# Patch tokens by row: the patch projection of an image and text transformer with the patches as the stationary operand

## The chip, the cores and the metric

One NeuronCore of a Trainium2 chip runs the whole kernel. The metric is the device time of one execution in microseconds. Of the kernel before, three executions are given; their median is 570.28 us. The profile of one further execution has a span (first to last instruction on the core) of 532.9 us.

## The reference

```python
h = tok_ref(x, W, b, cls_token, pos_enc)         # 64 images, 36 patches each of 3 x 16 x 16 = 768 values
#   proj = patches @ W.T + b; out = concat([cls, proj]) + pos_enc     -> (64, 37, 256)
h = concatenate([h, txt], axis=1)                # txt (64, 77, 256)   -> (64, 114, 256)
h = h + attn_ref(layernorm(h))                   # linear attention, 16 heads: Q, K = elu(.) + 1
h = h + ffn_ref(layernorm(h))                    # 8 experts, each token goes to its best one
```

All is float32. The patch projection is the part that is changed; what comes after it reads its result, a token in a row of 256 values, from the tile rows_all.

## The kernel before, in words

**Precision.** A float32 product is made of three matmuls: both operands are split into a high part (a cast, mostly on ScalarE) and a low part, the rest (a subtraction on VectorE, `low`, L778). `product` (L1078 to L1080) multiplies high by high, high by low and low by high.

**Patch stage.** The 64 images are worked on eight at a time (OCT), 288 patches, and each eight in two units, which hold three chunks of 128 of the 768 features each. There are 16 units. In a unit a 128 x 128 block of the weight is stationary and 288 patches move past it, so a token comes out as a column: features on the partitions. For a unit, SyncE loads `x_in` (a ring of four), ScalarE casts to `xp_hi` (L625, a ring of two), VectorE makes `xp_lo` (L778), TensorE makes 18 matmuls, and after each second unit VectorE adds position and bias out of PSUM into `tokT_all` (`patches_out`, L817), by columns. The two units of one eight share their PSUM banks.

**Into rows.** The attention needs tokens by rows, 114 of one image on 114 partitions: 36 patches, the class token at row 36, 77 texts. For each pair of images GpSimd copies the patch columns from `tokT_all` to `tokT` (L540), TensorE turns them in four transposes into the bank `b_tok` (L1237), and ScalarE copies these to `rows_all` (L722). The texts come by DMA straight into their rows (`load_text`, L409).

**Attention loop.** It goes over 32 pairs of images, in steps; a step i holds pieces of the pairs i + 3 (turning the patch tokens) to i - 4 (the scatter). On each engine the order within a step is written out by hand in its `step(i)`, the same code for the first steps, a hardware loop over steps 8 to 23 unrolled by four, and the last ones. In a step: statistics of the first layer norm (VectorE, L834 and L840), its reciprocal root on GpSimd (`rstd`, L495 to L500), the normalised xn on ScalarE (L696), its transposes (L1148), K and V (`kvp`), Q, `k_in` (VectorE, L961), `k_neg`, `k_relu`, `k_exp` (ScalarE, L684 to L687), `k_sb` (GpSimd, L550), `kvm` (L1135), `apply` (L1120), `attn` (VectorE, L896), its transposes (L1111), the output product `wo`, the residual (VectorE, L873), statistics of the second norm, `rstd` again on GpSimd, xn on ScalarE (L667), its transposes (L1211), a copy `xn2T` (ScalarE, L704), the gate product (L1248), the choice of the expert and the rank of each token (L1195 to L1198), and two indirect DMAs by GpSimd, which write each token's row to its expert's region in DRAM (`scatter`, L521). From step 24 on, the experts' weights are split in the same steps (GpSimd L562). GpSimd's order in a step is: `so_far`, the copy to `tokT`, `rstd` of the first norm, `k_sb`, `rstd` of the second norm, `scatter`. TensorE's is: `kvm`, xn transposes, attention transposes, K and V, `wo`, `apply`, ranks, xn2 transposes, Q, the four transposes of patch tokens, the gate product.

**Early steps.** Steps -3, -2 and -1 prepare the first pairs; they stand between units of the patch stage, at places written out in the `units` lists.

**Queues.** SyncE's program is one list of DMAs and waits, all in order: weights of the projection, units, small tensors, constants, other weights, texts of the first pairs; then the remaining units, each behind a wait for its ring slot; then texts, each behind a wait on the statistics of two pairs before. GpSimd splits the attention weights during the patch stage (L572 to L582).

**After the loop.** A table of tiles by expert is made, and 64 tiles of 128 tokens go through their expert and are written to the output by indirect DMA. The change does not touch this part.

## Time and profile before

| what | us |
|---|---|
| median of the three executions | 570.28 |
| lowest, highest | 568.74, 573.35 |
| span of the profiled execution | 532.9 |
| TensorE matmul busy | 478.5 (90%) |
| VectorE busy | 394.3 (74%) |
| GpSimd busy | 348.1 (65%) |
| ScalarE busy | 335.1 (63%) |

The device time of the profiled execution itself is not listed apart from its span; the median lies 37.4 us above the span. A matmul record covers the passage through the array, so that records of successive matmuls overlap: work is read from the distance of their starts. The patch stage takes the first 52 us, the attention loop lasts until about 400, and the expert tiles take the rest.

### The profile page before, as it was taken

The numbers are of one execution on the slowest core, as the hardware profiler recorded it, in microseconds if no ns is written. First come the engines' busy times: TensorE is split into PE (matmuls) and PEld (weight loads), VectorE is DVE, ScalarE is ACT, GpSimd is POOL, SyncE is SP. The second block draws the span as 40 slices with busy tenths as digits, with TensorE's granted clock in tenths as the row PEclk, the third lists the DMA queues.
The fourth block names the chain that finished last, engine by engine and source line by source line (L and its number), as shares of the span: only waits on it lengthen the run. The fifth ranks groups of instructions, "written<-read, shape, count | busy, mean of one in ns | idle before, by whom it ended". The sixth has DMA issues, their size and how long they took to land. (4 is left out here: it accounts for less than half of the span.)

```text
span 532.9 us, 13968 instructions
## 1 busy us (share of the span) xinstructions
PE 478.5 (90%) x3686; PEld 445.1 (84%) x3687; DVE 394.3 (74%) x1324; ACT 335.1 (63%) x805; POOL 348.1 (65%) x727
## 2 busy tenths in 40 slices
PE   4999899999999999999999999999954499999991
PEld 4988789999898999989999988888843498989990
DVE  4666478888887888788878877877854288888881
ACT  4334467667666757766676776766632488888870
POOL 0463234677777677777777778887776067877774
PEclk9999899999999999999999999999995599999996
DMA  8951000111121112711111211110013567852220
GB/s 298 281 168 34 14 23 14 39 35 33 34 56 33 30 37 81 238 30 51 39 30 36 55 31 31 42 35 22 18 38 99 155 196 220 241 160 82 78 79 31
DMA packets 31578, 43.24 MB, mean 81 GB/s; under 512 B 8541, under 2 KB 23840, under 8 KB 31539
## 3 DMA queue, kind: packets, MB, share of 16 engines
q1 hardware_dynamic: 21650, 27.12, 17.4%
q0 software_dynamic: 9216, 15.12, 8.9%
q10 hardware_dynamic: 672, 0.53, 0.3%
q8 instruction: 18, 0.29, 0.2%
q14 instruction: 22, 0.17, 0.1%
HBM read 26.45 MB, written 17.17 MB: 82 GB/s over the span
## 5 line engine op out<-in xcount | busy, mean ns | idle before, releaser
L521 POOL DMA_INDIRECT sorted_rows<-rows,place x64 | 75.1, 1174 | 39.7 <-POOL place L516 28.7
L608 POOL DMA_INDIRECT out<-result,result_id x64 | 62.6, 978 | 30.2 <-DVE result L1059 13.7
L684 ACT ACTIVATE k_neg<-k_in 114x512 f32<-114x512 f32 x32 | 20.3, 634 | 59.7 <-DVE k_in L961 59.7
L1078 PE MATMUL b_kvp<-wkv_hi,xnT_hi 128*114 128x512 f32 x128 | 52.9, 413 | 0.0
L696 ACT ACTIVATE xn<-rows_all,shift,rstd 114x256 f32<-114x256 f32 (+1 forms) x64 | 34.9, 593 | 27.6 <-issue 24.2
L498 POOL TENSOR_TENSOR rstd<-ve,half_neg 114x2 f32<-114x2 f32 x64 | 47.0, 734 | 5.3
L1079 PE MATMUL b_kvp<-wkv_lo,xnT_hi 128*114 128x512 f32 x128 | 50.4, 394 | 0.0
L1080 PE MATMUL b_kvp<-wkv_hi,xnT_lo 128*114 128x512 f32 x128 | 50.2, 392 | 0.0
L495 POOL TENSOR_SCALAR ve<-mv 114x2 f32<-114x2 f32 x64 | 15.3, 239 | 53.2 <-DVE mv L840 29.3
L550 POOL TENSOR_TENSOR k_sb<-k_exp,k_relu 114x512 f32<-114x512 f32 x32 | 41.2, 1287 | 5.8 <-issue 4.4
L1078 PE MATMUL b_kvp<-wgu_hi,xsT_hi 128*128 x128 | 37.7, 294 | 6.3 <-DVE xsT_lo L778 6.3
L766 ACT ACTIVATE xs<-rows_all,affine 128x256 f32 (+1 forms) x64 | 39.1, 611 | 6.5 <-DVE affine L1066 6.5
L1135 PE MATMUL b_att<-v_sb,k_sb 114*128 114x136 f32 x256 | 38.5, 294 | 3.1 <-POOL k_sb L550 3.1
L1078 PE MATMUL b_qo<-wo_hi,attnT_hi 128*114 128x256 f32 x128 | 41.0, 320 | 0.0
L1078 PE MATMUL b_qo<-xnT_hi,wq_hi 128*128 128x256 f32 x128 | 38.7, 303 | 0.0
L667 ACT ACTIVATE xn<-rows,shift,rstd 114x256 f32<-114x256 f32 x64 | 35.1, 602 | 4.5 <-POOL shift L500 4.5
L1248 PEld LDWEIGHTS b_gate<-gate_s,xn2T 128*114 128x114 f32 x256 | 29.6, 187 | 9.7 <-ACT xn2T L704 9.1
L1080 PE MATMUL b_kvp<-wgu_hi,xsT_lo 128*128 x128 | 36.4, 284 | 0.0
L1079 PE MATMUL b_kvp<-wgu_lo,xsT_hi 128*128 x128 | 36.4, 284 | 0.0
L1248 PE MATMUL b_gate<-gate_s,xn2T 128*114 128x8 f32 x256 | 31.1, 248 | 5.7 <-ACT xn2T L704 5.7
L1080 PE MATMUL b_qo<-xnT_hi,wq_lo 128*128 128x256 f32 x128 | 36.0, 281 | 0.0
L1079 PE MATMUL b_qo<-xnT_lo,wq_hi 128*128 128x256 f32 x128 | 35.9, 281 | 0.0
(174 smaller groups left out, 1771.3 us busy)
## 6 DMA issues: line engine op xcount, KB each, us to landing
rows_all<-sorted_rows SPq DMA_DIRECT2D x64, 130.0 KB
rows_all<-in_x SPq DMA_DIRECT2D x16, 432.0 KB, 4.8
rows_all<-in_txt SPq DMA_DIRECT2D x32, 154.0 KB
rows_all<-in_wgu SPq DMA_DIRECT2D x8, 256.0 KB, 4.5
sorted_rows<-rows,place POOLq DMA_INDIRECT x64, 3.7
rows_all<-in_wdown SPq DMA_DIRECT2D x8, 128.0 KB, 4.7
out<-result,result_id POOLq DMA_INDIRECT x64
rows_all<-in_w_tok SPq DMA_DIRECT2D x2, 384.0 KB, 4.1
```

What stands on the lines that cost most here:

```text
L498: G.tensor_tensor(to[:, k, :], ve[:, 0, :], half_neg[0:TOK, :], ALU.pow).then_inc(chain, 1)
L521: G.indirect_dma_start(out=scratch[0:EXPERTS * REGION, :], out_offset=bass.IndirectOffsetOnAxis(ap=place[:, k, b:b + 1], axis=0), in_=rows ...
L550: G.tensor_tensor(k_sb[:], k_exp[:], k_relu[:], ALU.add).then_inc(k_ready, 1)
L608: G.indirect_dma_start(out=out, out_offset=bass.IndirectOffsetOnAxis(ap=result_id[:, k:k + 1], axis=0), in_=result[:, k, :], in_offset=Non ...
L667: last = S.activation(xn2[:, b, :], rows[:, k, b, 0:D], ACT.Identity, bias=shift2[:, k, b:b + 1], scale=rstd2[:, k, b:b + 1])
L696: last = S.activation(xn[:, b, :], rows_all[0:TOK, bass.ds(2 * p.n + b, 1), 0:D], ACT.Identity, bias=shift1[:, p.slot(2), b:b + 1], scale= ...
L766: S.activation(xs[:, t.slot(4)], rows_all[:, bass.ds(t.n, 1), 0:D], ACT.Identity, bias=affine[:, t.slot(4), 0:1], scale=affine[:, t.slot(4 ...
L1078: T.matmul(to, left_hi, right_hi, start=start, stop=False)
L1079: T.matmul(to, left_hi, right_lo, start=False, stop=False)
L1080: return T.matmul(to, left_lo, right_hi, start=False, stop=stop)
L1135: last = T.matmul(b_att[:, b, c * KVW:(c + 1) * KVW], k_sb[:, b, c * P:(c + 1) * P], v_sb[:, b, c, :], start=True, stop=True)
L1248: last = T.matmul(b_gate[0:TOK, b * EXPERTS:(b + 1) * EXPERTS], xn2T[:, k, b * TOK:(b + 1) * TOK], gate_s[:, k, :], start=(k == 0), stop=( ...
```

## The change

The operands of the patch projection change places. 128 patches (of three and a half images) are stationary and the 256 output features move, so a token comes out as a row. There are 18 units of 128 patches and all 768 features. VectorE adds position and bias out of PSUM into `patch_out`, a ring of four; the sum of position and bias by patch, in nine tiles that repeat, is made by GpSimd from a larger input `pos`. A tile of 128 patches isn't aligned with images, so each is stored to a table in DRAM, `patch_rows`, and read back by pairs of images to its rows in `rows_all`, beside the texts (`load_pair`). The class token's row is added once and written to all images by two DMAs (`cls_rows`). The copy to `tokT`, the transposes and the copy out of `b_tok` are gone, with `tokT_all`, `tokT` and their semaphores. In the early steps, -3 is gone. The host's layout of `x`, `pos`, `tok_b` and `cls` changes accordingly.

```diff
@@ -220,7 +220,7 @@
 
 
         staging = rows_all[:, TILES // 2:, :].rearrange("p t w -> p (t w)")
-        X_UNIT = (FC // 2) * OCT * PATCHES
...
@@ -347,9 +349,9 @@
         id_copied = sem("id_copied")
         stored = [sem(f"stored{k}") for k in range(4)]
 
-        SMALL_DMAS, WEIGHT_DMAS = 5, 5
+        SMALL_DMAS, WEIGHT_DMAS = 4, 5
         CONST_DMAS = 2
...
@@ -390,6 +392,11 @@
                 else:
                     what()
 
+        def patch_bank(t):
+
+            bank = (b_kvp, b_att)[(t.c // 2) % 2]
+            return bank[:, t.c % 2, 0:D]
+
...
@@ -402,44 +409,84 @@
                     sp.wait_ge(x_lo_ready, u.upto(4))
                 sp.dma_start(x_in[:, k * X_UNIT:(k + 1) * X_UNIT], x[bass.ds(u.n, 1)]).then_inc(x_loaded[k], 16)
 
-            def load_text(p):
+            def load_pair(p):
 
                 if p.had(2):
                     sp.wait_ge(mv1_ready, p.upto(2))
                 sp.dma_start(rows_all[CLS_AT + 1:TOK, bass.ds(2 * p.n, 2), 0:D],
                              txt[:, bass.ds(2 * p.n, 2)]).then_inc(s_in[p.slot(2)], 16)
-
+                sp.dma_start(rows_all[0:PATCHES, bass.ds(2 * p.n, 2), 0:D],
+                             patch_images[:, bass.ds(2 * p.n, 2)]).then_inc(s_in[p.slot(2)], 16)
+
+            def store_patches(t):
+
+                k = t.slot(4)
+                sp.wait_ge(patches_ready, t.upto())
+                sp.dma_start(patch_rows[bass.ds(t.n * P, P), :], patch_out[:, k]).then_inc(patches_stored[k], 16)
+
+            def stored_patches(t):
+
+                sp.wait_ge(patches_stored[t.slot(4)], 16 * t.rounds(4))
+
+            def cls_rows(n):
+
+                half = slice(n * IMAGES // 2, (n + 1) * IMAGES // 2)
+                sp.dma_start(rows_all[CLS_AT:CLS_AT + 1, half, 0:D],
+                             cls_row[:].rearrange("p (a d) -> p a d", a=1).to_broadcast([1, IMAGES // 2, D])
+                             ).then_inc(s_cls_rows, 16)
+
+            patch_images = patch_rows.rearrange("(i n) d -> n i d", n=PATCHES)
             W_HALF = FC // 2 * D
             sp.dma_start(w_tok_raw[:, 0:W_HALF], w_tok[:, 0:W_HALF]).then_inc(s_tokw, 16)
             load_unit(Turn(0, 0))
             sp.dma_start(w_tok_raw[:, W_HALF:], w_tok[:, W_HALF:]).then_inc(s_tokw2, 16)
             load_unit(Turn(0, 1))
-            for to, what in ((pos_s, pos), (tokb_s, tok_b), (cls_s, cls), (bq_s, bq), (gate_s, gate)):
+            sp.dma_start(tokb_s[:], tok_b.to_broadcast([P, D])).then_inc(s_pos, 16)
+            for n in range(POS_PARTS):
+                at = slice(n * POS_TILES // POS_PARTS, (n + 1) * POS_TILES // POS_PARTS)
+                sp.dma_start(posb[:, at], pos[:, at]).then_inc(s_pos, 16)
+                if n < 2:
+                    load_unit(Turn(0, 2 + n))
+            for to, what in ((cls_s, cls), (cls_pos_s, cls_pos), (bq_s, bq), (gate_s, gate)):
                 sp.dma_start(to[:], what).then_inc(s_small, 16)
-            for n in (2, 3):
-                load_unit(Turn(0, n))
+            load_unit(Turn(0, 4))
             sp.dma_start(con_s[:], consts).then_inc(s_const, 16)
             sp.dma_start(ids_s[:], ids).then_inc(s_const, 16)
-            load_unit(Turn(0, 4))
+            load_unit(Turn(0, 5))
+            store_patches(Turn(0, 0))
+            sp.wait_ge(s_cls, 1)
+            cls_rows(0)
             sp.dma_start(wkv_raw, wkv).then_inc(s_weights, 16)
-            load_unit(Turn(0, 5))
+            load_unit(Turn(0, 6))
+            store_patches(Turn(0, 1))
+            stored_patches(Turn(0, 0))
+            load_pair(Turn(0, 0))
+            load_unit(Turn(0, 7))
+            store_patches(Turn(0, 2))
+            stored_patches(Turn(0, 1))
+            load_pair(Turn(0, 1))
             sp.dma_start(wq_raw, wq).then_inc(s_weights, 16)
             sp.dma_start(wo_raw, wo).then_inc(s_weights, 16)
             sp.dma_start(bkv_s[:], bkv.to_broadcast([TOK, 2 * D])).then_inc(s_weights, 16)
             sp.dma_start(bias_row[:], bo).then_inc(s_weights, 16)
-            load_unit(Turn(0, 6))
-            for n in (0, 1):
-                load_text(Turn(0, n))
-            load_unit(Turn(0, 7))
-            with sp.Fori(2, UNITS // 4) as m:
-                for c in range(4):
-                    load_unit(Turn(m, c))
+            for n in range(8, PT):
+                load_unit(Turn(0, n))
+                store_patches(Turn(0, n - 5))
+            for n in range(PT - 5, PT):
+                store_patches(Turn(0, n))
+            sp.wait_ge(w_lo, 2)
+            sp.wait_ge(x_lo_ready, PT)
+            sp.wait_ge(weight_step, 6)
+            cls_rows(1)
+            for n in range(PT - 4, PT):
+                stored_patches(Turn(0, n))
+            sp.wait_ge(s_cls_rows, 32)
             for n in (2, 3):
-                load_text(Turn(0, n))
+                load_pair(Turn(0, n))
             BEFORE_EXPERTS = GU_STEP // 4 - 1
             with sp.Fori(1, BEFORE_EXPERTS) as m:
                 for c in range(4):
-                    load_text(Turn(m, c))
+                    load_pair(Turn(m, c))
             sp.wait_ge(h2_ready, RAW_PAIRS)
             for e in range(EXPERTS):
                 at = e * (GU + DOWN)
...
@@ -531,13 +578,6 @@
                         pool.wait_ge(rank_done, p.upto(1))
                     G.tensor_tensor(so_far[0:TOK, (p + 1).slot(2)], so_far[0:TOK, p.slot(2)], chosen[:, p.slot(2)],
                                     ALU.add).then_inc(so_far_ready, 1)
-                if (i + 3).within(PAIRS):
-                    p = i + 3
-                    until = ahead(pool, p.upto(1))
-                    pool.wait_ge(s_prep, 1)
-                    if p.had(1):
-                        pool.wait_ge(back_done, until)
-                    G.tensor_copy(tokT[:, :, :, 0:PATCHES], tokT_all[:, :, bass.ds(2 * p.n, 2), :]).then_inc(tokT_ready, 1)
...
@@ -562,9 +602,12 @@
                     G.tensor_tensor(wgu_lo[:, e].rearrange("p k d -> p (k d)"), expert_raw[:, at:at + GU],
                                     wgu_hi[:, e].rearrange("p k d -> p (k d)").bitcast(F32), ALU.subtract).then_inc(gu_lo_ready, 1)
 
-            pool.wait_ge(s_prep, 1)
-            pool.wait_ge(patches_ready, 1)
-            step(Turn(0, -3))
+            pool.wait_ge(s_pos, 16 * (POS_PARTS + 1))
+            for n in range(POS_PARTS):
+                at = slice(n * POS_TILES // POS_PARTS, (n + 1) * POS_TILES // POS_PARTS)
+                G.tensor_tensor(posb[:, at], posb[:, at],
+                                tokb_s[:].rearrange("p (a d) -> p a d", a=1).to_broadcast([P, POS_TILES // POS_PARTS, D]),
+                                ALU.add).then_inc(pos_ready, 1)
 
             pool.wait_ge(s_weights, 16 * WEIGHT_DMAS)
...
@@ -714,13 +756,6 @@
                         S.activation(q_exp[:, c, :], at, ACT.Exp, bias=bq_s[:, c:c + 1])
                         last = S.activation(q_relu[:, c, :], at, ACT.Relu, bias=bq_s[:, c:c + 1])
                     last.then_inc(q_parts, 1)
-                if (i + 3).within(PAIRS):
-                    p = i + 3
-                    until = ahead(act, p.upto())
-                    act.wait_ge(s_small, 16)
-                    act.wait_ge(back_done, until)
-                    S.activation(rows_all[0:PATCHES + 1, bass.ds(2 * p.n, 2), 0:D],
-                                 b_tok[0:PATCHES + 1, :].rearrange("p (b d) -> p b d", b=2), ACT.Copy).then_inc(h_ready, 1)
 
             def w_tok_part(h, arrived):
...
@@ -737,8 +772,7 @@
 
             units(act, unit, [
                 lambda: w_tok_part(0, s_tokw), 0, lambda: w_tok_part(1, s_tokw2), 1,
-                2, 3, "steady", lambda: step(Turn(0, -3)), 12, bias_rows, 13,
-                14, lambda: step(Turn(0, -2)), 15, lambda: step(Turn(0, -1))])
+                2, 3, "steady", bias_rows, lambda: step(Turn(0, -2)), 16, 17, lambda: step(Turn(0, -1))])
             walk(act, BEFORE_A, STEADY_A, AFTER_A, step)
             zero_tails(act, range(EXPERTS // 2, EXPERTS))
             S.activation(silu_ahead[:], bq_s[:, 0:1], ACT.Silu)
...
@@ -810,15 +841,14 @@
                     last = V.tensor_copy(so_far[:, k], con["c_region"].rearrange("p (b e) -> p b e", b=2))
                 last.then_inc(s_posb, 1)
 
-            def patches_out(q, k):
-
-                dve.wait_ge(unit_done, 2 * q + 2)
-                for c, bank in enumerate((b_kvp, b_att)):
-                    last = V.tensor_tensor(
-                        tokT_all[:, c, bass.ds(OCT * q, OCT), :],
-                        bank[:, k, 0:OCT * PATCHES].rearrange("p (b n) -> p b n", b=OCT),
-                        posb[:, c:c + 1, :].to_broadcast([P, OCT, PATCHES]), ALU.add)
-                last.then_inc(patches_ready, 1)
+            def patches_out(t):
+
+                dve.wait_ge(unit_done, t.upto())
+                if t.n * POS_PARTS < POS_TILES * POS_PARTS:
+                    dve.wait_ge(pos_ready, t.n * POS_PARTS // POS_TILES + 1)
+                if t.had(4):
+                    dve.wait_ge(patches_stored[t.slot(4)], 16 * t.rounds(4, 4))
+                V.tensor_tensor(patch_out[:, t.slot(4)], patch_bank(t), posb[:, t.n % POS_TILES], ALU.add).then_inc(patches_ready, 1)
 
             def unit(u):
...
@@ -826,8 +856,8 @@
                 dve.wait_ge(x_hi_ready, u.upto())
                 low(xp_lo[:, u.slot(2)].rearrange("p f n -> p (f n)"), x_in[:, k * X_UNIT:(k + 1) * X_UNIT],
                     xp_hi[:, u.slot(2)].rearrange("p f n -> p (f n)")).then_inc(x_lo_ready, 1)
-                if u.c % 2 == 0 and u.had(2):
-                    patches_out(2 * u.m + u.c // 2 - 1, (u.c // 2 - 1) % 2)
+                if u.had(2):
+                    patches_out(u - 2)
 
             def stats(src, to, mv, done, ready, p):
                 for b in range(2):
...
@@ -850,9 +880,10 @@
 
             def stats_1(p):
 
-                until, until2, until3 = ahead(dve, p.upto()), ahead(dve, 16 * p.rounds(2)), ahead(dve, p.upto(2))
+                until2, until3 = ahead(dve, 32 * p.rounds(2)), ahead(dve, p.upto(2))
                 dve.wait_ge(s_posb, 2)
-                dve.wait_ge(h_ready, until)
+                if not p.had(1):
+                    dve.wait_ge(s_cls_rows, 16)
                 dve.wait_ge(s_in[p.slot(2)], until2)
                 if p.had(2):
...
@@ -996,14 +1027,15 @@
 
             def room_setup():
 
-                patches_out(UNITS // 2 - 1, (UNITS // 2 - 1) % 2)
+                for n in (PT - 2, PT - 1):
+                    patches_out(Turn(0, n))
                 dve.wait_ge(s_bias_dma, 48)
                 V.memset(v_sb[:, :, :, P:], 1.0)
                 V.memset(rows[:, :, :, ID + 1:], 0.0).then_inc(room_ready, 1)
 
             units(dve, unit, [
-                lambda: w_tok_part(0), 0, lambda: w_tok_part(1), 1, position, 2, 3, tables, "steady",
-                12, lambda: step(Turn(0, -2)), 13, 14, 15, lambda: step(Turn(0, -1)), room_setup])
+                lambda: w_tok_part(0), 0, lambda: w_tok_part(1), 1, position, 2, 3, tables, *range(4, 14),
+                lambda: step(Turn(0, -2)), 14, 15, 16, 17, lambda: step(Turn(0, -1)), room_setup])
             walk(dve, BEFORE_A, STEADY_A, AFTER_A, step)
 
...
@@ -1081,17 +1113,15 @@
 
             def unit(u):
 
-                if u.fixed and u.n < 2:
-                    pe.wait_ge(w_lo, u.n + 1)
+                xk = u.slot(2)
+                if u.had(4):
+                    pe.wait_ge(patches_ready, u.upto(4))
                 pe.wait_ge(x_lo_ready, u.upto())
-                if u.c % 2 == 0 and u.had(4):
-                    pe.wait_ge(patches_ready, 2 * u.m + u.c // 2 - 1)
-                for c, bank in enumerate((b_kvp, b_att)):
-                    for k in range(FC // 2):
-                        f = (u.c % 2) * (FC // 2) + k
-                        w, xk = slice(c * P, (c + 1) * P), u.slot(2)
-                        last = product(bank[:, (u.c // 2) % 2, 0:OCT * PATCHES], (w_tok_hi[:, f, w], w_tok_lo[:, f, w]),
-                                       (xp_hi[:, xk, k, :], xp_lo[:, xk, k, :]), f == 0, f == FC - 1)
+                for f in range(FC):
+                    if u.fixed and u.n == 0 and f % (FC // 2) == 0:
+                        pe.wait_ge(w_lo, f // (FC // 2) + 1)
+                    last = product(patch_bank(u), (xp_hi[:, xk, f, :], xp_lo[:, xk, f, :]),
+                                   (w_tok_hi[:, f, :], w_tok_lo[:, f, :]), f == 0, f == FC - 1)
                 last.then_inc(unit_done, 1)
 
...
@@ -1222,20 +1250,6 @@
                             last = product(b_qo[:, c * QW:(c + 1) * QW], (wq_hi[:, k, w], wq_lo[:, k, w]),
                                            (xnT_hi[:, p.slot(2), k, :], xnT_lo[:, p.slot(2), k, :]), k == 0, k == KC - 1)
                     last.then_inc(q_done, 1)
-                if (i + 3).within(PAIRS):
-                    p = i + 3
-                    until, until2 = ahead(pe, p.upto()), ahead(pe, p.upto(7 if p.had(7) else 1))
-                    pe.wait_ge(s_posb, 1)
-                    pe.wait_ge(tokT_ready, until)
-                    if p.had(7):
-                        pe.wait_ge(place_ready, until2)
-                    elif p.had(1):
-                        pe.wait_ge(h_ready, until2)
-                    for b in range(2):
-                        for c in range(KC):
-                            at = b * D + c * P
-                            last = T.transpose(b_tok[0:PATCHES + 1, at:at + P], tokT[:, c, b, :], ident)
-                    last.then_inc(back_done, 1)
                 if (i - 3).within(PAIRS):
                     p = i - 3
```

## Rows read from the trace of the kernel before

**Rows 1.** Stretches of the span: length, then busy us of each engine, TensorE clock, DMA share, GB/s.

```profile
0.00:10.00 10.00, 2.81 (x12) 2.85 (x14) 4.85 (x13) 4.77 (x5) 0.19 (x4) 1.00 0.78 262
10.00:20.00 10.00, 10.00 (x69) 9.86 (x69) 5.44 (x18) 3.27 (x4) 0.31 (x1) 1.00 1.03 338
60.00:64.00 4.00, 3.98 (x17) 3.70 (x18) 1.79 (x3) 1.92 (x5) 0.22 (x1) 0.58 0.00 0
80.00:300.00 220.00, 219.47 (x1729) 202.88 (x1728) 178.75 (x605) 150.37 (x340) 158.26 (x371) 1.00 0.17 51
```

**Rows 2.** Who waited for whom, 80 to 300 us: total us, times, longest.

```profile
PEld b_gate L1248 <- ACT xn2T L704: 1.7, 5, 0.8
```

**Rows 3.** Timeline of TensorE in one step: start us, us, what.

```profile
255.50 0.70 PE L1248 MATMUL b_gate<-gate_s,xn2T 128*114 128x8 f32 x6
...
265.29 0.28 PE L1080 MATMUL b_qo<-xnT_hi,wq_lo 128*128 128x256 f32 x1
265.41 0.60 PE L1237 MATMUL b_tok<-con_s,tokT 128*37 128x128 f32 x4
265.94 0.96 PE L1248 MATMUL b_gate<-gate_s,xn2T 128*114 128x8 f32 x8
```

**Rows 4.** Timeline of ScalarE in the same step.

```profile
264.37 1.10 ACT L696 ACTIVATE xn<-rows_all,shift,rstd 114x256 f32 x2 [0.85 <-issue]
265.37 0.52 ACT L704 COPY xn2T<-b_turn 128x456 f32<-128x456 f32 x1
```

**Rows 5.** Timeline of GpSimd in the same step.

```profile
255.90 0.23 POOL L495 TENSOR_SCALAR ve<-mv 114x2 f32<-114x2 f32 x1 [0.88 <-DVE mv L840]
...
262.18 0.30 POOL L540 COPY tokT<-tokT_all 128x144 f32 x1
262.56 0.23 POOL L495 TENSOR_SCALAR ve<-mv 114x2 f32<-114x2 f32 x1
...
264.17 1.29 POOL L550 TENSOR_TENSOR k_sb<-k_exp,k_relu 114x512 f32<-114x512 f32 x1
266.25 0.23 POOL L495 TENSOR_SCALAR ve<-mv 114x2 f32<-114x2 f32 x1 [0.80 <-DVE mv L840]
```

**Rows 6.** k_neg and wgu_lo by line (min/median/max ns, first and last start), then ScalarE.

```profile
L684 ACT ACTIVATE k_neg<-k_in x32: 632/634/637, 56.9 to 379.2; 114x512 f32<-114x512 f32 x32
...
L562 POOL TENSOR_TENSOR wgu_lo<-rows_all,wgu_hi x8: 1277/1292/1300, 313.9 to 389.7; 128x512 fp32r<-128x512 f32 x8
...
318.38 0.52 ACT L704 COPY xn2T<-b_turn 128x456 f32<-128x456 f32 x1
...
329.50 0.52 ACT L704 COPY xn2T<-b_turn 128x456 f32<-128x456 f32 x1
```

**Rows 7.** DMA landings: line of in_x (min/median/max us), then issues with KB, median us.

```profile
DMA to landing us min/median/max: 3.0/4.8/7.9
...
sorted_rows<-tail_rows SPq DMA_DIRECT2D x5, 130.0 KB, 3.0
```

**Rows 8.** Patch stage: timelines of TensorE and ScalarE, and the subtraction by line.

```profile
8.05 0.44 PE L1078 MATMUL b_kvp<-xp_hi,w_tok_hi 128*128 128x288 f32 x1
...
18.02 0.29 PE L1078 MATMUL b_att<-xp_hi,w_tok_hi 128*128 128x288 f32 x1
...
18.42 0.30 PE L1078 MATMUL b_att<-xp_hi,w_tok_hi 128*128 128x288 f32 x1
...
22.23 0.92 ACT L625 CAST xp_hi<-rows_all 128x864 fp32r<-128x864 f32 x1 [1.85 <-PE b_att L1080]
...
L778 DVE TENSOR_TENSOR xp_lo<-rows_all,xp_hi x14: 1024/1060/2093, 13.0 to 47.5; 128x864 fp32r<-128x864 f32 x14
```

**Rows 9.** Start of the attention loop: timelines of TensorE and VectorE.

```profile
51.26 0.29 PE L1080 MATMUL b_att<-xp_hi,w_tok_lo 128*128 128x288 f32 x1
...
60.02 0.82 PE L1135 MATMUL b_att<-v_sb,k_sb 114*128 114x136 f32 x2 [2.02 <-POOL k_sb L550]
...
56.17 0.69 DVE L961 TENSOR_TENSOR k_in<-b_kvp,bkv_s 114x512 f32<-114x512 f32 x1 [0.56 <-PE b_kvp L1080]
```

67 lines of the change are left out of this document (32 added, 35 removed).

## The prediction

> **What bounds the kernel now.** I read the page first, then the stretches by stage, then who waits for whom, and then single instructions of one step of the attention loop. Between 80 and 300 us TensorE is busy 219.5 of 220 us at full clock, with VectorE at 179, GpSimd at 158 and ScalarE at 150 [rows 1]. That looks like a kernel bound by TensorE, so that every matmul taken away is won. But the row that counts is another: in the same stretch the weight load of the gate product waits for ScalarE's xn2T [rows 2], seldom by much, because matmul records overlap and hide gaps below 0.3 us. One step shows it. The last q product starts at 265.29, the four transposes of patch tokens are one group from 265.41, and the gate product starts at 265.94 [rows 3]. xn2T ends on ScalarE at 265.37 + 0.52 = 265.89 [rows 4]. So the gate product starts 0.05 us after xn2T, and the transposes ahead of it (four at about 0.11, 0.44 us) lie in front of a wait.
>
> What does xn2T wait for? It comes behind xn on ScalarE, which starts at 264.37 [rows 4], 0.18 after GpSimd's shift has ended at about 264.19 (k_sb starts next, at 264.17). That shift ends the short chain of the first layer norm, begun at 262.56, which GpSimd could not begin earlier: since 255.90 it had been through the second layer norm, the fields of the scatter, two indirect DMAs, and at 262.18 the copy to tokT [rows 5]. The chain begun at 255.90 was released by VectorE's statistics, as its successor at 266.25 was (0.80 us idle ahead of it, released by mv). These statistics come at the end of the run kvm, turn, kvp, wo, residual that starts with the gate product at 255.50 [rows 3].
>
> So there is a loop through three engines: gate product to GpSimd, 255.50 to 266.25, 10.75 us; GpSimd to the gate product, 255.90 to 265.94, 10.04 us. A lap is 20.8 us and covers two steps: 10.4 a step. k_neg comes 32 times from 56.9 to 379.2, 322.3 / 31 = 10.40 us a step [rows 6]. The kernel also has its own test of it: from step 24 GpSimd has one more instruction of 1.29 us a step, about 1.37 with its gap. A loop of two steps should lengthen by half of this, 0.69; xn2T at 318.38 and 329.50 shows 11.12 a step [rows 6], 0.72 more. TensorE has no more work in these steps. The bound is the loop.
>
> **The change, term by term.** The profiled execution has a span of 532.9 us; the median of the runs is 570.28, so 37.4 us lie around the span. I make the sum against 532.9 and add the same 37.4, as nothing in the change speaks of what lies outside.
>
> *Loop steps, transposes.* 32 x 4 transposes go, 0.44 us a step. They stand between q and the gate product, where TensorE then waits longer for xn2T. Costed at nothing; the cover is the loop. If it were gone they would be worth 29 x 0.44 = 12.8 us (rival A).
>
> *Loop steps, GpSimd.* The copy to tokT goes. From its start to that of the next instruction it holds GpSimd 262.56 - 262.18 = 0.38 us [rows 5], and this is on the loop. One lap has it once and is two steps long, so a step gains 0.19. The loop binds from about step 5 to 28: 24 x 0.19 = 4.6 us. In the first five steps the loop is still filling and TensorE has less to do; there I give the transposes about half of their 5 x 0.44, 1.0. Gain 5.6. What is late next: TensorE needs about 9.9 us a step (255.50 to 265.41) without the transposes, so 10.2 is still the loop's.
>
> *Loop steps, ScalarE.* The copy of b_tok to rows_all goes. It stands at the end of a step, and what follows it, tanh and xnT_hi, waits for TensorE's gate product and turn. ScalarE, busy 150 of 220 us, only idles longer there. Nothing. The wait of the rank product on h_ready becomes one on place_ready of the pair before, some 8 us old by then: nothing.
>
> *Loop steps, SP.* Each pair now brings a second DMA (72 KB) behind the text, under the same wait on mv1 of two steps before. stats_1 needs it about two steps (20 us) later against a landing of 3 to 5 us [rows 7]; SP does nothing else there. Nothing, unless that cover goes.
>
> *Patch stage, TensorE.* Now 18 units of 18 products with 256 moving columns for 16 units of 18 with 288. Starts at full clock are 0.133 us apart at 288 (18.02 to 18.42 is three) [rows 8] and 0.12 at 256 (265.29 to 265.41) [rows 3]: 324 x 0.119 = 38.6 against 288 x 0.133 = 38.3, +0.3. Casting and subtracting move as many elements as before: 0.92 and 1.06 us at 864 columns [rows 8] become 0.82 and 0.94 at 768. With two buffers of xp the next unit is ready 1.8 to 1.9 us after the unit two before it is done, and a unit takes 2.14: tight, but covered as before, also where GpSimd's splitting of weights stretches the subtraction to 2.09 [rows 8].
>
> *Patch stage, the new inputs.* pos grows to three pieces of 393 KB, tok_b to 131 KB, and the small tensors now queue behind them. Bytes up to these: w_tok 0.79, units 0 to 3 1.57, pos and tok_b 1.31, together 3.67 MB. The first 10 us move 2.62 MB (262 GB/s) and the next ten 338 GB/s [rows 1]; so 13.1 us, 13.4 with the small ones. VectorE's position() blocks there, with the low half of unit 2 queued behind it: 0.4 + 0.94 us, so unit 2 starts at about 14.8. TensorE is done with unit 1 at about 13.5 (first product at 7.2; the records of the first products are 0.44 us long against 0.30 later [rows 8], half clock, for some 5 us). +1.3. GpSimd's three additions of 768 elements cost 1.29 x 768 / 512 = 1.93 each [rows 5], the first ends at 15.4 and holds patches_out(0), behind which the low half of unit 3 is queued: +0.3.
>
> *Patch stage, SP.* Its queue is a list by hand. store_patches(0) waits for the addition (15.8); then wkv, unit 6, store 1, a wait until store 0 has landed, pair 0, unit 7, store 2, a wait for store 1, pair 1, the other weights, and only then unit 8. With some 0.45 us an issue and 4.8 a landing in this crowded stretch [rows 7], unit 8 is issued at about 24.8. Landed after 3.0 to 4.8 us and converted in 1.8, it starts at 29.6 to 31.4; TensorE would be there at 28.0. Middle: 2.5, I take +2.4, bounds 0 and 6 (each store landing in 7.9). The loads after it have four buffers and catch up. Two of the early transposes and the ScalarE copy ahead of the last cast go: -0.5. Patch stage together: 0.3 + 1.3 + 0.3 + 2.4 - 0.5 = +3.8. Its last product ends at 51.55 now [rows 9], at about 55.4 after.
>
> *Start of attention.* Now k_in of pair 0 starts at 56.17, 4.6 us after the last product [rows 9]. After, VectorE has stats_1 of pair 2 ahead of k_in, and pair 2 comes through DRAM only after the last unit is stored, since SP waits for the last four stores and only then issues pair 2. From the last product: additions 0.65, store 3.0 (130 KB to DRAM land in 3.0) [rows 7], issue of two DMAs 0.45, landing 3.0 (the least of the x loads), statistics 1.1: 8.2, so +3.6. The cls row's second half and the splitting of weights are covered by the store. This trace has no DRAM write followed by a read of it; the bounds are 2 (both landings overlapped with kvp as far as they can be) and 7 (4.8 each). The Trainium skill (DMA: Bandwidth & Descriptors, Anatomy of one DMA) gives a DMA a fixed cost of about 2.0 us plus its bytes, mostly the write receipt, heaviest in DRAM. By that, 2.3 and 2.2 us, this term would be an estimated +2.1 and the sum +0.8. I keep the rows.
>
> TensorE waits meanwhile. Ahead of 60.02 it idles for 2.0 us now, and in 60 to 64 its mean clock is 0.58 [rows 1, 9]: 1.2 GHz for a time after the idle. A longer idle gives somewhat more of it: +0.5, bounds 0 and 3.
>
> *After the loop.* The drain, the tables and the expert tiles are unchanged: nothing.
>
> Sum: -5.6 + 3.8 + 3.6 + 0.5 = +2.3. Span 535.2, time 572.6.
>
> **Rivals.** *A, TensorE is the bound.* For it: 219.5 of 220 us busy [rows 1]. Against: the 0.05 us behind xn2T [rows 3, 4] and the 11.12 of the expert steps. It gives -12.8 + 7.9 = -4.9, about 565.4; with no stall for units 2 and 8 (-4.0), 561.4. The Trainium skill (Trainium Kernel Development and Optimization, Best Practices) says to judge the distance to the roofline by weight-load busy and not matmul busy. That is 202.9 of 220 here, still the highest of all, so by that rule too TensorE would be taken for the bound and this time expected. Chance 0.17, with what else would end faster by over 1%.
>
> *B, slower: the SP queue starves the patch stage.* Place: unit 7 and unit 8, each behind a wait for a store's landing. Price: with 7.9 us, the longest landing of the rows [rows 7], for stores 0 and 1, units 7 and 8 come 3 and 6 us late, and GpSimd's weight splitting moves later and stretches subtractions that before were covered. Patch stage +8 rather than +3.8, attention start +5: net +7.9, 578. It decides from landings of about 6 us under load. For it: in 10 to 20 us the DMA share is 1.03 [rows 1] before anything is added. Chance 0.35.
>
> *C, the loop gains less:* another chain (k_sb, which follows the same shift, or the second DMA of a pair) takes it over. Then -2 in place of -5.6: 576.2. Within 1% by itself; it adds weight to B.
>
> *D, the change does not do what it says:* transposes remain somewhere. The diff leaves none on patch tokens; 0.01.
>
> **How the numbers follow.** A measurement of this kernel can tell about 1%, 5.7 us, from no change. My own forecast, 567 to 576, has 0.47. B ends at 576 to 582, A at 561 to 566. The range is 564.5 to 580.5: it takes in the bounds of the store's path and of unit 8. Faster 0.17, within 1% 0.48, slower 0.35.
>
> **What would show it.** The step (k_neg to k_neg) goes from 10.40 to about 10.2; 9.96 would be rival A, 10.4 rival C. The gate product's wait for xn2T grows to about 0.3 us a step. The last patch product ends near 55.4, with holes ahead of units 2 and 8. k_in of pair 0 starts 8 us behind it, released by a DMA into rows_all through the statistics. From the table to the end nothing changes. I am wrong if the step falls by more than 0.3, or if the patch stage ends beyond 58.

## The result, and the profile after

The changed kernel takes 578.57 us (median of four executions, 576.5 to 579.84) where the kernel before takes 569.62 in the same comparison: ratio 1.0176, interval [1.0109, 1.0243]. It is slower by 9 us. (A ratio here leaves out the executions that lie more than 1.5% above the fastest of the same kernel; a median is of all.) The forecast of 572.6 lay within 1%, so the likeliest of the three cases, within 1%, was the wrong one, though the time is inside the range and close to that of rival B.

The profiled execution took 577.74 us and has a span of 575.7. So 2.0 us lie around the span, not 37.4 as the prediction assumed; where those 37 us are comes below. First the loop. The stretches, in the columns of [rows 1] (in 0 to 10 us the clock column says 1.00, but the first products there start 0.21 us apart, which is half clock):

```profile
0.00:10.00 10.00, 3.15 (x14) 3.17 (x16) 4.29 (x9) 4.61 (x5) 0.19 (x4) 1.00 0.77 224
10.00:20.00 10.00, 2.88 (x24) 2.67 (x23) 4.38 (x8) 1.66 (x2) 4.65 (x3) 0.85 0.73 277
...
38.00:44.00 6.00, 5.13 (x24) 5.13 (x25) 3.21 (x5) 1.40 (x2) 5.78 (x5) 0.50 0.58 190
66.00:80.00 14.00, 7.67 (x41) 6.84 (x42) 4.15 (x10) 4.54 (x10) 2.61 (x5) 0.82 0.25 67
80.00:300.00 220.00, 216.43 (x1643) 196.75 (x1641) 180.18 (x602) 142.98 (x316) 146.23 (x335) 1.00 0.20 58
```

In 80 to 300 TensorE is still busy nearly all the time. From 10 to 20 us it was busy 10.0 of 10 and is now busy 2.9: half of what the patch stage loses is lost there.

The wait of the gate product for xn2T over 80 to 300 (it was 1.7 us, five times [rows 2]), then one step on TensorE and on ScalarE:

```profile
PEld b_gate L1262 <- ACT xn2T L746: 5.3, 16, 0.8
```

```profile
248.47 0.28 PE L1112 MATMUL b_qo<-xnT_hi,wq_lo 128*128 128x256 f32 x1
248.91 0.96 PE L1262 MATMUL b_gate<-gate_s,xn2T 128*114 128x8 f32 x8 [0.17 <-ACT xn2T L746]
...
248.34 0.52 ACT L746 COPY xn2T<-b_turn 128x456 f32<-128x456 f32 x1
```

xn2T ends at 248.86 and the gate product starts 0.05 later, as in [rows 3, 4]. The transposes ahead of it are gone, and TensorE waits in their place. On GpSimd nothing stands any more between so_far and the chain of the first norm, where the copy to tokT was [rows 5]:

```profile
255.39 0.23 POOL L579 TENSOR_TENSOR so_far<-so_far,chosen 114x16 bf16<-114x16 bf16 x1
255.70 0.23 POOL L542 TENSOR_SCALAR ve<-mv 114x2 f32<-114x2 f32 x1
...
257.28 1.28 POOL L590 TENSOR_TENSOR k_sb<-k_exp,k_relu 114x512 f32<-114x512 f32 x1
```

k_neg, one a step, for comparison with [rows 6]:

```profile
L726 ACT ACTIVATE k_neg<-k_in x32: 630/633/635, 74.0 to 392.1; 114x512 f32<-114x512 f32 x32
```

It first comes 17.1 us later (56.9 before) and last 12.8 later (379.2): the loop as a whole takes 318.1 us for 322.3.

Now the patch stage. VectorE, GpSimd and TensorE around unit 2 (GpSimd's three additions of one row took 1.79, 1.98 and 2.54 us, from 15.35, 17.11 and 19.05):

```profile
15.68 1.74 DVE L830 TENSOR_TENSOR cls_row<-cls_s,cls_pos_s 1x256 f32<-1x256 f32 x1 [5.58 <-DMA gate_s<-in_gate]
...
17.72 2.19 DVE L812 TENSOR_TENSOR xp_lo<-rows_all,xp_hi 128x768 fp32r<-128x768 f32 x1
...
20.16 2.25 DVE L812 TENSOR_TENSOR xp_lo<-rows_all,xp_hi 128x768 fp32r<-128x768 f32 x1
...
15.35 6.24 POOL L608 TENSOR_TENSOR posb<-posb,tokb_s 128x768 f32<-128x768 f32 x3 [14.94 <-DMA posb<-in_pos]
...
19.96 0.58 PE L1110 MATMUL b_att<-w_tok_hi,xp_hi 128*128 128x256 f32 x1 [7.12 <-DVE xp_lo L812]
...
20.55 0.41 PE L1112 MATMUL b_att<-w_tok_hi,xp_lo 128*128 128x256 f32 x1
20.77 0.41 PE L1110 MATMUL b_att<-w_tok_hi,xp_hi 128*128 128x256 f32 x1
```

Unit 2 waits for its low half, which stands behind VectorE's cls_row, and this for a small tensor that landed at 15.6. An addition of 256 values on one partition then takes 1.74 us and the subtraction 2.19 instead of 0.96. The matmuls of the unit start 0.21 us apart rather than 0.12: after 7.1 us without work, TensorE runs the unit at half clock.

The second hole, ahead of unit 8 (SyncE's issues, ScalarE, GpSimd, VectorE, TensorE):

```profile
29.43 0.28 SPq L471 DMA_DIRECT2D bias_row<-in_bo  x1
29.76 0.37 SPq L410 DMA_DIRECT2D rows_all<-in_x  x1
...
36.53 0.83 ACT L668 CAST xp_hi<-rows_all 128x768 fp32r<-128x768 f32 x1 [5.09 <-DMA rows_all<-in_x]
...
35.68 0.39 POOL L615 CAST bias_part<-bias_row 1x256 bf16<-1x256 f32 x1 [14.08 <-DMA bias_row<-in_bo]
...
37.40 1.42 DVE L812 TENSOR_TENSOR xp_lo<-rows_all,xp_hi 128x768 fp32r<-128x768 f32 x1 [4.63 <-ACT xp_hi L668]
...
38.87 0.58 PE L1110 MATMUL b_kvp<-w_tok_hi,xp_hi 128*128 128x256 f32 x1 [3.97 <-DVE xp_lo L812]
```

Unit 8's load is issued at 29.76, behind the weights, and lands 6.7 us later; the clock of 38 to 44 us is 0.50. At the end of the stage and the start of attention [rows 9]:

```profile
65.18 0.28 PE L1112 MATMUL b_kvp<-w_tok_hi,xp_lo 128*128 128x256 f32 x1
...
72.29 0.75 DVE L864 BATCH_NORM_STATS2 stats<-rows_all 114x6 f32<-114x256 f32 x2 [4.15 <-DMA rows_all<-patch_rows]
...
73.31 0.66 DVE L992 TENSOR_TENSOR k_in<-b_kvp,bkv_s 114x512 f32<-114x512 f32 x1
```

The last patch product starts at 65.18 and not at 51.26 (+13.9); k_in of pair 0 follows 8.1 us behind it, behind the statistics of pair 2, which come through DRAM.

**Where the 37 us are.** The 64 expert tiles, by VectorE's row for each, in the kernel before and after:

```profile
L1066 DVE COPY affine<-rows_all x64: 157/159/418, 418.6 to 514.2; 128x2 f32 x48, 128x2 f32<-128x2 f32 x16
```

```profile
L1098 DVE COPY affine<-rows_all x64: 153/159/447, 431.7 to 555.8; 128x2 f32 x48, 128x2 f32<-128x2 f32 x16
```

95.6 us against 124.1, in code that the change doesn't touch. Here seventeen of the tiles come more than 2.4 us behind the one ahead of them, fourteen of these by 3 to 4.1 us, where 1.4 is the rule; in the profile of the kernel before six do, none by 3. That profile came from an execution without these stalls. The executions that gave 570 will have had them: the runs below show 536 us for the same kernel in a session whose profiles have none, and 570 in sessions whose profiles, all of changed kernels, have them. The kernel before was not itself profiled in such a session, so how its 34 us are shared out is not shown; in the changed kernels the tiles account for 29 to 33. So a span against a span does not compare the two kernels; points ahead of the tiles do.

| start of | before | after | difference |
|---|---|---|---|
| last patch product | 51.26 | 65.18 | +13.9 |
| k_neg of pair 0 | 56.90 | 74.00 | +17.1 |
| k_neg of pair 31 | 379.24 | 392.05 | +12.8 |
| first expert tile | 418.64 | 431.72 | +13.1 |

### The profile page after: what moved, and what is told of

It is laid out like the page before. It is cut to its first block, busy times and chain, and to the rows that moved or that the text cites. A ratio compares the mean times of both kernels' runs of the same rounds, so it can differ in the third digit from the quotient of the medians.

```text
span 575.7 us, 13646 instructions
## 1 busy us (share of the span) xinstructions
PE 481.7 (84%) x3594; PEld 440.6 (77%) x3595; DVE 396.3 (69%) x1323; ACT 322.1 (56%) x775; POOL 340.8 (59%) x698
## 4 chain that ended last, share of the span: by engine, by line
PE 42%; issue 13%; POOL 10%; DVE 10%; ACT 7%; DMA 1%; POOLq 1%; DVEq 1%; another core or an unknown queue 1%; ACTq 0%; SPq 0%
PE b_kvp L1112 6%; PE b_att L1165 5%; PE b_kvp L1110 5%; PE b_gate L1262 4%; PE b_kvp L1111 4%; POOL sorted_rows L568 2%; PE b_turn L1178 2%; ACT xn L738 2%; PE b_att L1150 2%; DVE stats L864 2%; PE b_qo L1110 2%; DVE attnT_lo L812 2%; PE b_qo L1111 2%; PE b_qo L1112 2%; ACT xnT_hi L699 2%
## 5 line engine op out<-in xcount | busy, mean ns | idle before, releaser
L738 ACT ACTIVATE xn<-rows_all,shift,rstd 114x256 f32<-114x256 f32 (+1 forms) x64 | 34.9, 593 | 24.0 <-issue 21.8
L1075 DVE TENSOR_TENSOR act_u<-b_kvp,silu_g 128x128 f32<-128x128 f32 x64 | 18.5, 289 | 35.8 <-ACT silu_g L784 23.7
L784 ACT ACTIVATE silu_g<-b_kvp 128x128 f32<-128x128 f32 x64 | 17.7, 276 | 42.9 <-PE b_kvp L1112 35.9
L1165 PEld LDWEIGHTS b_att<-v_sb,k_sb 114*128 114x128 f32 x256 | 32.8, 195 | 8.1 <-POOL k_sb L590 8.1
```

The source lines that it names most:

```text
L738: last = S.activation(xn[:, b, :], rows_all[0:TOK, bass.ds(2 * p.n + b, 1), 0:D], ACT.Identity, bias=shift1[:, p.slot(2), b:b + 1], scale= ...
L1165: last = T.matmul(b_att[:, b, c * KVW:(c + 1) * KVW], k_sb[:, b, c * P:(c + 1) * P], v_sb[:, b, c, :], start=True, stop=True)
```

## The experiments

Twelve runs followed, in three sessions; two of them, e1 and e5, have no edit. The kernel before took 536.34, 569.38 and 570.53 us in them (medians of 7, 19 and 31 executions), so ratios are to it within a session, and profiles are compared by the points of the table above.

**First session. e1, the kernel before once more.** No edit.

> The kernel before, unchanged, profiled once more. The profile shown of it has a span of 532.9 us beside timed runs of 569 to 573, the profile after one of 575.7 beside 577.7. Theory 1: that profiled execution lacked stalls of 1.2 to 2 us, all engines at once, which the profile after shows between 430 and 560 us, and an ordinary execution of the kernel before has them too. Then the span here is about 567, the first 64 tile statistics (affine 0 to 63) take about 124 us as after and not 95.5, and the attention loop is as shown (10.4 us a step). Rival: the stalls belong to the change; then the span here is about 533 and the tiles take 95.5 us.

533.52 us, span 531.7, last patch product 51.89, k_neg of pair 31 at 378.2, tiles 95.3 us. Theory 1 missed and the rival's numbers came, but not its reason: in the first session the kernel before has no stalls in the tiles, and neither had the three variants of the changed kernel that follow (their tiles 95.4 to 96.1 us). In the second session all tiles took 125 to 128 us. The third session ran on the chip of the first, and there they took 125 to 129 and the kernel before 570. So the stalls belong to the session, not to the change, and not to one chip. What makes them stays open.

**e2, the copy back on GpSimd.** The changed kernel, with a copy as large as the one to tokT in its old place, of data that nobody uses.

```
+ if (i + 3).within(PAIRS) ...:        # its waits are left out here
+     G.tensor_copy(copied[:], con_s[:, 0:144])
```

> The kernel after, with a copy of 128x144 on GpSimd put back at its old place in each step (its result is used by nobody). Theory (the loop through GpSimd, ScalarE and TensorE sets the step, one lap in two steps): the step between k_neg 8 and 23 goes from 10.25 back to about 10.45, the whole is 4.5 us slower than the kernel after. Rival (TensorE sets the step): the step stays at 10.25 and the time does not move, since TensorE gets no work.

```profile
L734 ACT ACTIVATE k_neg<-k_in x32: 629/632/635, 72.4 to 400.5; 114x512 f32<-114x512 f32 x32
```

The step from pair 8 to 23 is 10.49 us, for 10.25 without the copy and 10.46 in the kernel before. The loop takes 328.1 us rather than 318.1, but not all of these 10 us are the copy's: in the last seven steps TensorE's clock fell three times here and not once in the first profile of the changed kernel (see the loop's sum below), which makes 3 to 4 us. Ratio 1.0334 [1.0279, 1.039].

**e3, four transposes back on TensorE**, in their old place, of a constant, with nothing behind them.

```
+ for n in range(4):                   # condition, waits and at are left out here
+     T.transpose(b_tok[0:PATCHES + 1, at:at + P], con_s[:, 0:PATCHES + 1], ident)
```

> The kernel after, with four transposes of 37 columns put back on TensorE at their old place in each step, ahead of the gate product (their result is used by nobody), and nothing on GpSimd or ScalarE. Theory (the loop sets the step): they lie in front of the wait for xn2T, the step stays at 10.25 and the time within 1 us of the kernel after. Rival (TensorE sets the step): 0.44 us a step, 10.69, and 13 us slower.

```profile
L726 ACT ACTIVATE k_neg<-k_in x32: 630/633/635, 73.1 to 393.9; 114x512 f32<-114x512 f32 x32
```

Step 10.34, where the theory said 10.25 and the rival 10.69: 0.09 us of the 0.44 that they take. Ratio 1.0247 [1.0202, 1.0292]. The first stages are those of the changed kernel, and its loop would be 2 to 3 us shorter (31 x 0.09), so an estimate of what the change costs where the tiles have no stalls is 10 to 13 us. With e2 it settles the loop: GpSimd's 0.38 us are worth 0.24 a step, TensorE's 0.44 are worth 0.09. (The two together give more than the 0.21 that the change took away, so each is good to about a tenth.)

**e4, the small tensors first.** The changed kernel, with SyncE issuing cls, cls_pos, bq and gate ahead of tok_b and pos.

```
+ for to, what in ((cls_s, cls), (cls_pos_s, cls_pos), (bq_s, bq), (gate_s, gate)): ...
  sp.dma_start(tokb_s[:], tok_b.to_broadcast([P, D]))
  for n in range(POS_PARTS): ...
- for to, what in ((cls_s, cls), ...
```

> The kernel after, with the four small loads (cls, cls_pos, bq, gate) issued ahead of tok_b and pos. Theory (VectorE stood at position() from 10.1 to 15.7 us for them, with the low half of unit 2 behind): unit 2 starts at about 14 instead of 19.96; unit 3 still waits for the first addition of position and bias on GpSimd, behind patches_out(0), and starts at about 20 instead of 23.9. The last patch product is 4 us earlier. Rival (the crowd of DMAs sets these units anyhow, or the addition on GpSimd): unit 2 comes earlier but unit 3 does not, and the last patch product stays within 1 us of 65.2.

```profile
8.59 0.40 DVE L830 TENSOR_TENSOR cls_row<-cls_s,cls_pos_s 1x256 f32<-1x256 f32 x1
...
12.74 0.96 DVE L812 TENSOR_TENSOR xp_lo<-rows_all,xp_hi 128x768 fp32r<-128x768 f32 x1 [3.48 <-ACT xp_hi L668]
17.07 2.14 DVE L812 TENSOR_TENSOR xp_lo<-rows_all,xp_hi 128x768 fp32r<-128x768 f32 x1
...
19.27 0.58 PE L1110 MATMUL b_att<-w_tok_hi,xp_hi 128*128 128x256 f32 x1 [3.10 <-DVE xp_lo L812]
```

Away from GpSimd's additions cls_row takes 0.40 us and not 1.74, and the subtraction 0.96. The hole ahead of unit 2 is gone. A hole of 3.1 us ahead of unit 3 takes its place, whose subtraction waits for the first addition (patches_out of unit 0 stands ahead of it) and then takes 2.14. The last product comes at 59.32 rather than 64.2, as the theory had it. Ahead of unit 8, whose load is issued earlier since the first store is, the hole is now 2.8 us. Ratio 1.0153 [1.0106, 1.0201].

**Second session. e5, the changed kernel once more**, as the measure for the next three.

> The kernel after, unchanged, on the same chip as the runs beside it: the base for the other edits. In the first comparison the expert tiles took 124 us after with stalls of all engines, and in e2 to e4, whose tiles are the same code, 96. Theory: the stalls belonged to that chip or session and hit both kernels. Then the tiles (affine 0 to 63) take 96 here, the last patch product starts at 64 to 65, and the time is 10 to 13 us above the kernel before. Rival: without the stalls the kernels are within 1%, 541 or less.

Last product 64.20, k_neg of pair 0 at 72.97, of pair 31 at 394.37, tiles 124.9 us. The tiles were expected at 96 and have the stalls. Median 581.23, 11.9 us above that of the kernel before, ratio 1.0091 [1.0023, 1.016]. This ratio rests on the four lowest of ten executions, one of them far below the rest; the medians give 1.021. Its interval overlaps that of the first comparison.

**e6, unit 8's load earlier.** The waits for the stores' landings, and pairs 0 and 1, go behind the loads of units 8 to 10; one store stands between two loads.

```
  store_patches(Turn(0, 1))
- stored_patches(Turn(0, 0)); load_pair(Turn(0, 0))
  load_unit(Turn(0, 7))
  store_patches(Turn(0, 2))
- stored_patches(Turn(0, 1)); load_pair(Turn(0, 1))
+ load_unit(Turn(0, 8)); store_patches(Turn(0, 3))
  ... wq, wo, bkv, bo
+ load_unit(Turn(0, 9)); store_patches(Turn(0, 4)); stored_patches(Turn(0, 0)); load_pair(Turn(0, 0))
+ load_unit(Turn(0, 10)); store_patches(Turn(0, 5)); stored_patches(Turn(0, 1)); load_pair(Turn(0, 1))
```

> The kernel after, with SyncE's list in another order: units 7 and 8 are loaded before it waits for the landing of stores 0 and 1, the other weights before pairs 0 and 1, these two pairs after units 9 and 10. Theory (unit 8 starts 4.0 us late since its load stands behind two waits for landings, two pairs and four weights, and GpSimd's splitting starts late for the same reason): the hole ahead of unit 8 closes and TensorE's clock does not fall there, the last patch product is 5 us earlier than in the kernel after. Rival (DMA bandwidth is the bound there, whatever the order): hole and time stay within 1 us.

```profile
38.34 0.38 PE L1116 MATMUL b_kvp<-w_tok_hi,xp_hi 128*128 128x256 f32 x1 [1.09 <-DVE xp_lo L818]
42.84 0.39 PE L1116 MATMUL b_att<-w_tok_hi,xp_hi 128*128 128x256 f32 x1 [2.09 <-DVE xp_lo L818]
...
36.40 0.83 ACT L674 CAST xp_hi<-rows_all 128x768 fp32r<-128x768 f32 x1 [2.62 <-DMA rows_all<-in_x]
39.05 0.83 ACT L674 CAST xp_hi<-rows_all 128x768 fp32r<-128x768 f32 x1 [1.82 <-DMA rows_all<-in_x]
...
39.92 2.87 DVE L818 TENSOR_TENSOR xp_lo<-rows_all,xp_hi 128x768 fp32r<-128x768 f32 x1 [1.29 <-ACT xp_hi L674]
```

Unit 8 starts at 34.9 without a hole and at full clock, so the order of SyncE's list made that hole. But TensorE now waits 1.1 and 2.1 us for units 9 and 10: their loads are late in turn, and the subtraction of unit 10 takes 2.87 us beside GpSimd's splitting. The last product comes at 62.43, 1.8 earlier and not 5. Median 579.48, ratio 1.0144 [1.0083, 1.0205]: the time does not tell it from e5.

**e7, pairs 2 and 3 earlier.** SyncE issues them when unit 2's store has landed and not behind the last four stores and the second half of the class rows. patch_out moves out of the space that they share.

```
  for n in range(PT - 5, PT):
      store_patches(Turn(0, n))
+     if n == PT - 5: stored_patches(Turn(0, 2)); load_pair(Turn(0, 2))
+     if n == PT - 3: load_pair(Turn(0, 3))
```

> The kernel after, with pairs 2 and 3 read back from DRAM as soon as their own patches are stored and the statistics of pairs 0 and 1 are made, ahead of the last stores, not behind the landing of the last four (patch_out gets room of its own for this). Theory (k_in of pair 0 stands on VectorE behind the statistics of pair 2, which wait for that DRAM round trip): k_in of pair 0 comes about 5 us behind the last patch product rather than 8, and the time is 3 us better. Rival (something else, such as xn of pair 1 on GpSimd and ScalarE, holds kvp up anyway): less than 1 us.

```profile
68.38 0.74 DVE L867 BATCH_NORM_STATS2 stats<-rows_all 114x6 f32<-114x256 f32 x2
...
70.03 0.69 DVE L995 TENSOR_TENSOR k_in<-b_kvp,bkv_s 114x512 f32<-114x512 f32 x1 [0.56 <-PE b_kvp L1115]
```

k_in is released by its product again, and the statistics are done ahead of it. k_neg of pair 0 stands 5.2 us behind the last product and not 8.8. There is a second gain: TensorE's idle ahead of the first kvm is 2.5 us and not 6.0, its clock does not fall there, and pair 1 follows pair 0 by 8.25 us and not 10.63. Pair 31 at 389.3 for 394.4, though the last product is 1.3 later than in e5. Median 576.48, 4.8 below e5, ratio 1.0104 [1.0038, 1.017].

**e8, the edits of e4, e6 and e7 together.**

> The kernel after, with the three edits together: small loads first, SyncE's list reordered, pairs 2 and 3 early. If the three holes add up: 4 + 5 + 3 = 12 us better than the kernel after, level with the kernel before or up to 2 us better (the step of 10.25 against 10.45 is worth 4.5 us, the rest of GpSimd's additions and the splitting costs 2 to 4). Rival (they overlap, the crowd of DMAs only moves): 6 us better and still slower than before.

Last product 59.57, k_neg of pair 0 at 64.82 (8.15 earlier than e5), of pair 31 at 383.5 (10.9 earlier, where 12 were expected). Median 571.89, 9.3 below e5, ratio 1.0024 [0.9967, 1.0081]: level with the kernel before. Left over are holes ahead of unit 3 (3.1 us), 9 and 10 (1.7 and 2.2).

**Third session: what makes the holes that are left.** All four kernels start from e8.

**e9, position added one unit later**, so that unit 3's subtraction does not stand behind the wait for GpSimd.

```
- if u.had(2): patches_out(u - 2)
+ if u.had(3): patches_out(u - 3)
```

> On top of the kernel with all three edits (last product 59.6, k_neg of pair 0 at 64.8, of pair 31 at 383.5), VectorE adds the position to a unit three units later, not two, so that the subtraction of unit 3 no longer stands behind the wait for GpSimd's addition. Theory 1 (TensorE's 3.3 us hole ahead of unit 3 is this order): unit 3 starts right behind unit 2, at about 16.0 and not 19.3; the subtraction of unit 4 then runs beside GpSimd's additions (2.1 us and not 0.96) and opens a hole of about 1 us of its own; last product -2 us, at 57.5, pair 31 -2. Theory 2 (the loads of units 9 and 10 and GpSimd's splitting of weights set the later units, whatever comes before): unit 3 earlier, but the holes ahead of units 9 and 10 grow by as much, last product within 0.7 of 59.6.

```profile
18.00 1.43 DVE L848 CAST earlier<-con_s 114x114 bf16<-114x114 f32 x1
19.35 1.87 DVE L850 CAST so_far<-con_s 128x16 bf16<-128x16 f32 x2
21.13 0.94 DVE L821 TENSOR_TENSOR xp_lo<-rows_all,xp_hi 128x768 fp32r<-128x768 f32 x1
...
14.03 0.39 PE L1119 MATMUL b_att<-w_tok_hi,xp_hi 128*128 128x256 f32 x1 [0.22 <-DVE xp_lo L821]
22.13 0.38 PE L1119 MATMUL b_kvp<-w_tok_hi,xp_hi 128*128 128x256 f32 x1 [3.53 <-DVE xp_lo L821]
```

Both theories missed. Unit 3 follows unit 2 at once, but now all casts of the tables, 0.2 us without company, run beside the additions and take 1.43 and 1.87 (two of them); unit 4 waits 3.5 us for them. Its subtraction starts at 21.13, and at 21.10 in e8: in either order VectorE comes out of the additions when they end, at about 21. Each load from unit 6 on stands behind a store in SyncE's list, stores are a unit later, and the hole ahead of unit 9 grows from 1.7 to 3.2. Last product 62.51, 2.9 later than e8. Median 573.7, ratio 1.006 [1.0021, 1.0098].

**e10, the weights ahead of the first store.** SyncE stood idle there from 10 to 17 us.

```
  load_unit(Turn(0, 5))
+ wkv, wq, wo, bkv, bo                # their five dma_starts, moved up
  store_patches(Turn(0, 0))
```

> On top of the same three edits, SyncE issues the five attention weights and biases ahead of the first store (at about 10 us, when it stands idle) and not at 18 to 27 us. GpSimd then splits them from about 21 us and not from 32. Theory 1 (VectorE's subtraction beside GpSimd's splitting takes 1.3 to 3.0 us for 0.96, and this opens the holes of 1.8 and 2.4 us ahead of units 9 and 10): these holes go, holes of about the same sum open ahead of units 4 to 7, where the additions also end later; last product within 1 us of 59.6. Theory 2 (the splitting costs only where the loads are late too, as the kernel before has it at 20 to 34 us with holes of 0.5 to 0.9): holes at 9 and 10 go and less than 1.5 us comes in their place; last product -2.5, at 57.

```profile
22.84 0.39 POOL L624 CAST bias_part<-bias_row 1x256 bf16<-1x256 f32 x1 [1.94 <-DMA bias_row<-in_bo]
...
27.30 2.99 POOL L634 TENSOR_TENSOR wkv_lo<-rows_all,wkv_hi 128x1024 fp32r<-128x1024 f32 x1
...
28.39 2.72 DVE L821 TENSOR_TENSOR xp_lo<-rows_all,xp_hi 128x768 fp32r<-128x768 f32 x1
```

The splitting runs from 22.8 to 35.5. Subtractions beside it still take up to 2.7 us, but the holes ahead of units 9, 10 and 12, together 4.7, are gone, and 2.3 come in their place at units 6, 7 and 9 (0.8 each). Last product 57.39, 2.2 earlier: nearer to theory 2. Median 567.51, ratio 0.9942 [0.9902, 0.9981]. This is the one complete kernel that was measured faster than the kernel before, by 0.6%, which is less than the 1% that the prediction took to be tellable. Its k_neg of pair 31, at 381.3, is still 2 us behind that of [rows 6], which comes from another session, so the profiles don't show where its 3 us come from.

**e11, both.**

> The three edits, the addition of the position one unit later, and the weights ahead of the first store. If the holes are as the theories 1 of the two single runs have them: last product 57 to 58, k_neg of pair 0 at 62.5, pair 31 at 381.5, within 3 us of the kernel before there (378.2), ratio about 1.00. If the splitting costs nothing away from late loads: last product 55, pair 31 at 379, ratio 0.995.

Last product 57.76, no better than e10 alone; where 57 to 58 or 55 were expected; pair 31 at 383.4, 2 us worse. k_neg of pair 1 comes 9.85 us behind that of pair 0, and 8.25 in e10: the clock of 66 to 70 us is 0.57 here and 1.00 there, after the same idle of 2.5 us. Median 571.05, ratio 1.002 [0.9967, 1.0072].

**e12, no addition.** On top of e8, GpSimd adds tok_b to 8 values of each piece only. The kernel leaves out the projection's bias for nearly all features; it is there to price the additions.

```
- G.tensor_tensor(posb[:, at], posb[:, at], tokb_s[:]..., ALU.add)
+ G.tensor_tensor(posb[:, n * 3, 0:8], posb[:, n * 3, 0:8], tokb_s[:, 0:8], ALU.add)
```

> The three edits, and GpSimd adds tok_b to 8 values of each piece of pos and not to 9 x 256 (the projection's bias is left out for nearly all features). This prices GpSimd's three additions (1.8, 1.8 and 2.5 us, from 14.8 to 20.9). Theory 1 (they cost the path: 1.8 us of the wait ahead of unit 3, and the subtraction of unit 3 at 2.14 for 0.96 us): unit 3 starts at about 16.8 and not 19.3, last product -2.5. Theory 2 (the arrival of pos at 14.8 is the cause, the additions only fill the time): unit 3 at 18.5 or later, last product within 0.7 of 59.6.

```profile
15.30 0.95 DVE L819 TENSOR_TENSOR xp_lo<-rows_all,xp_hi 128x768 fp32r<-128x768 f32 x1
...
16.31 0.39 PE L1117 MATMUL b_att<-w_tok_hi,xp_hi 128*128 128x256 f32 x1 [0.27 <-DVE xp_lo L819]
```

```profile
66.00:70.00 4.00, 4.00 (x16) 3.54 (x16) 2.25 (x5) 0.96 (x3) 0.00 (x0) 0.50 0.00 0
```

Unit 3 starts at 16.3 and not at 19.3, and the last product comes at 57.20, 2.4 earlier, as theory 1 had it. So the additions cost 3.0 us at unit 3, and holes further on take 0.6 of it. The loop starts at half clock here (second row: 66 to 70 us), which costs 3.0 us by pair 1, and 1.6 come back in the last seven steps, so only 1.1 of the 2.4 is left at pair 31. Median 567.52, ratio 0.9955 [0.9911, 0.9999].

## Why the prediction was right or wrong, point by point

**The loop, GpSimd: right.** 0.19 a step was forecast. The step fell by 0.21 (10.46 to 10.25 from pair 8 to 23; 10.45 and 10.25 in e1 and e5), and e2 gave back 0.24. The gate product's wait grew to 5.3 us in 21 steps, 0.25 a step for the 0.3 forecast.

**The loop, transposes: nearly right.** Costed at nothing; e3 says 0.09 of 0.44. Rival A is out: a loop bound by TensorE would have stepped at 9.96. TensorE was the busiest engine both by matmuls (219.5 of 220) and by weight loads (202.9), and neither made it the bound.

**The loop's sum.** -5.6 forecast, less 0.5 for the clock. The loop gained 4.3 from the first k_neg to the last. What is missing lies in the last seven steps (pair 24 to 31), where 75.9 us became 75.4 and not some 74.6. And this profile was a lucky one. In ten profiles with this same step code the seven steps took 75.4 and 75.5 us (the first profile and e9), 76.5 once (e12) and 78.1 to 78.6 seven times; in both of the kernel before 75.9. The granted clock tells them apart. GpSimd splits the experts' weights there, and TensorE, with its transposes gone, idles 1.0 to 1.5 us ahead of some gate products (0.7 to 1.0 before). In the two short ones the clock never falls, in e12 it falls once, in the seven long ones twice, and each time a step of 12.7 to 14.2 us takes the place of one of 11.2 to 11.5, in part made up in the next. In e5 (columns of [rows 1]):

```profile
354.00:358.00 4.00, 4.00 (x20) 3.81 (x20) 2.55 (x7) 1.72 (x6) 2.70 (x9) 0.57 0.00 0
378.00:382.00 4.00, 4.00 (x19) 3.63 (x18) 2.94 (x8) 2.02 (x6) 2.57 (x7) 0.57 0.05 7
```

So in most of the profiles some 3 us of what the change wins at GpSimd are lost again at the loop's end, to a clock that had no term there. Whether it falls the idle alone doesn't decide: the first profile and e9 have idles of 1.0 to 1.4 us too. With full clock throughout, the loop takes 320.7 us before (e1) and 316.1 after (e9): 4.6 gained.

**Patch stage: the step that failed.** +3.8 forecast at the last product, +13.9 measured; by the prediction's own sign (beyond 58 us, and it is 65) it was wrong here. The places were right, holes ahead of units 2 and 8; their sizes were not. By its terms:

- *Unit 2*, "+1.3", became 7.4 - 0.1 = 7.3. Unit 2 started 5.2 us later than forecast, and TensorE was done with unit 1 0.8 earlier. The wait was under-priced twice. The small tensors landed at 15.6 where 13.4 was worked out from the bytes, and VectorE then ran beside GpSimd's additions. The prediction had that stretching for the weight splitting [rows 8] but not for the additions that it was itself pricing at 1.93 each: cls_row cost 1.3 more and the subtraction 1.2 more. e4 shows both. These three make 4.7 of the 5.2.
- *Unit 3*, "+0.3", cost nothing in the changed kernel, since unit 2 covered it. Its real size, 3.1, came out in e4, and e12 took 3.0 of it away.
- *Unit 8*, "+2.4", became 4.1. The load was issued at 29.8 and not at 24.8, since store 0 went out at 20.3 and not at 15.8, and it took 6.7 us to land, not 3.0 to 4.8. So most of the miss is unit 2's again: VectorE adds unit 0's position behind the subtraction that was late. In e4, without that, the hole is 2.8, close to the forecast. e6 shows that the order of the list makes it, but also that it is worth only 1.8 by itself.
- *Clock in the patch stage* was no term at all. After each of the two holes TensorE ran a unit or more at 1.2 GHz: unit 2 took 3.8 us for 2.0, unit 8 as much. Together about 3.6. The prediction had the clock only at its first products and ahead of the attention loop.

From the distances of all patch products: the holes grew by about 11.1 us in sum, the matmuls at half clock by 2.6 (the kernel before has some too, at its start), the work itself by 0.5, and the first product starts 0.3 earlier. That is the 13.9.

**SyncE's queue.** The forecast had rival B decide "from landings of about 6 us". Unit 8's was 6.7, and the time is B's, but its mechanism is only a part of it: stores 0 and 1 landed in 1.7 and 3.9 us, not in 7.9, and the larger hole was unit 2's. That the number fits B's 578 is in part luck. So is that it lies inside the range: the point of pair 31 moved by 12.8 us for a forecast of 2.3, and in e5's session the medians are 11.9 apart, which is outside.

**Start of attention: right.** +3.6 forecast, +3.2 measured (k_neg of pair 0 stands 8.8 us behind the last product, 5.6 before), and e7 took 3.6 back. One detail was wrong: not the store was last but the second half of the class rows, issued at 66.4 behind the stores and landed at 69.2; SyncE went on to pair 2 at 69.4. For the store I took the 3.0 us of the tail rows; the last ones landed in 1.7. The 2.3 that I estimated from the Trainium skill (DMA: Bandwidth & Descriptors, Anatomy of one DMA, a section on DMAs that GpSimd issues, where SyncE issues these) was the nearer of the two.

**Idle ahead of the loop, clock +0.5.** TensorE was busy 7.7 of 14 us in 66 to 80, at a clock of 0.82. Pair 1 follows pair 0 by 10.44 us, and by 9.85 in the profile before: +0.6, where 0.5 was forecast. But the clock had fallen there before the change too. With full clock it is 8.25, in e1 (the kernel before, after the same idle of 2.0 us) as in e7 to e10, so the idle of 6 us costs 2.2, and e7 won it back.

**After the loop: right for the change, wrong for the sum.** Nothing was forecast, and the tiles without stalls do not differ (95.3 and 95.5 us before, 95.4 to 96.1 in e2 to e4); with stalls only changed kernels were profiled. But 37.4 us were put around the span of which 2 lie there; most of the rest will be stalls in the tiles. The forecast survived since it added them as a constant. They may not be quite constant: in the sessions with stalls the tiles took 124 to 126 us when they began at 428 to 434 (after, e5 to e7), and 125 to 129 when they began at 420 to 423 (e8 to e12). So some 2 of the 13 us may have been given back there, and 9 us (first comparison) to 12 (medians of e5's session) measured and not 13. But e9's tiles, begun at 423, took 124.6, and no run took the stalls away within a session, so this is not shown.

**The rule on interference.** In the changed kernel cls_row starts at 15.68 and ends at 17.42, 0.28 after GpSimd's first addition. The subtraction started at 17.72 ends at 19.91, 0.82 after the second; the one started at 20.16 ends 0.82 after the third. And GpSimd's third addition, which ran while a subtraction ended, took 2.54 rather than 1.79. In e12, without the additions, the subtraction of unit 3 takes 0.95. Not every instruction of VectorE is held: the addition of position, which reads one input from PSUM, took 0.41 us at 19.83 beside the third addition, as it does elsewhere. This is the picture of a lock: one of the two waits for the other's instruction to end and then runs at its own speed. The Trainium skill says just this (SBUF — State Buffer, SBUF: two separate sides): VectorE, in an operation with two SBUF inputs, and GpSimd, in one that reads SBUF, share a port pair as an exclusive lock. Priced by it, each of the two VectorE instructions ahead of unit 2 would have got up to 1.8 us more; the measured sum is 2.6. The casts of e9 have one input and came out long too, which this rule of two inputs doesn't cover.

## What to carry to other kernels

An operation added on GpSimd in a crowded start must be priced at what VectorE has to do in the same microseconds: a subtraction, an addition or a cast of VectorE from SBUF can come out longer by nearly a whole instruction of GpSimd, whatever its own size. Where loads are issued from one list by hand, a new table belongs behind everything small that somebody waits for, and a hole that is closed shows the next one (here 7, 3, then 2 us), so price the whole list and not the load that is late. And a hole on TensorE can have a second price, the work behind it at half clock: in these runs units 2, 3, 4 and 8 had it behind 3.1 to 7.1 us of idle, and others behind some 2 us in one run and not in another. The same goes for a loop from which TensorE's filling work is taken: look at its idle ahead of the wait and at the clock behind it, in more than one profile.

## What the hardware showed that was not expected

- **Stalls that belong to a session.** The tiles, in code that no run changed, took 95 or 125 us on the same chip, half an hour apart. In a stall TensorE, VectorE and ScalarE all stand for over a microsecond while the DMA queues go on. Two of them in the changed kernel (columns of [rows 1]):

```profile
472.45:473.65 1.20, 0.12 (x2) 0.00 (x0) 0.00 (x0) 0.00 (x0) 0.80 (x2) 1.00 0.69 206
479.20:480.30 1.10, 0.14 (x2) 0.00 (x0) 0.00 (x0) 0.00 (x0) 0.82 (x2) 1.00 0.10 34
```

- **The clock after a short idle is not fixed by it.** After the same 2.5 us of idle ahead of the first kvm, the loop began at 1.00 in e10 and at 0.50 to 0.57 in e11 and e12, and 1.6 to 3.0 us were lost by pair 1. The kernel before did both, 0.58 in one profile and 1.00 in the other, after 2.0 us. What decides it these runs don't show.
- **A store to DRAM with a read of it behind** is cheap where the queues are not crowded: in the changed kernel the 128 KB stores from 39 us on land in 1.7 to 2.7 us, and 384 KB loads beside them in 3.1 to 3.8. From 30 to 34 us, with weights and loads in flight, three stores took 6.6 to 6.8 and the loads 6.7 to 7.1. The read of pair 2's rows (72 KB), issued at 69.75 in the changed kernel, had landed by 72.29.
